# Two-layer graph kernel: 128 rows in each indirect transfer, the basis weight as innermost index, and seven instead of eight dense units in the middle stage

## What is computed

```python
h = relu(layernorm(x))
# layer 0: spline convolution, nine basis weights for each edge, mean over the edges of a destination
basis = hat(edge_attr[:, 0])[:, :, None] * hat(edge_attr[:, 1])[:, None, :]       # E x 9
msg = einsum("ek,ei,kio->eo", basis, h[src], weight)                               # E x 32
x = x + segment_sum(msg, dst) / max(degree, 1) + h @ root_w.T + root_b
# layer 1: graph attention with 8 heads (edges and self loops), then a dense block
h = relu(layernorm(x))
g = gat(h, src, dst)                       # softmax over the edges of a destination, mean of heads
y = layernorm(g + bias_gat + h)
x = x + layernorm(relu(y @ w1 + b1) @ w2 + b2 + y)
```

## Time and profile before

| | |
|---|---|
| median of 3 runs | 3093.12 us (3092.24 to 3096.14) |
| profiled execution, its own time | 3089.18 us |
| its span | 3087.3 us |
| granted TensorE clock, mean | 0.812 |
| busy: PE, PEld, DVE, ACT, POOL | 2138.2, 1492.6, 1802.5, 852.1, 2468.6 us |
| indirect transfers on POOL | 800 + 400 + 400 + 400 |
| software DMA queue (q0) | 64000 packets, 30.57 MB |
| hardware DMA queue (q1) | 52070 packets, 91.52 MB |

### The profile page before, as it was taken

One profiled execution on the slowest core, in us unless ns is written; L12 is line 12 of the kernel. 1 busy time (PEld: TensorE's weight loads), 2 busy tenths in 40 slices (PEclk: granted clock), 3 DMA queues, 4 the chain that ended last, 5 costly groups with the idle time before them and its releaser, 6 DMA issues.

```text
span 3087.3 us, 33471 instructions
## 1 busy us (share of the span) xinstructions
PE 2138.2 (69%) x10666; PEld 1492.6 (48%) x10666; DVE 1802.5 (58%) x3234; ACT 852.1 (28%) x1616; POOL 2468.6 (80%) x2011
## 2 busy tenths in 40 slices
PE   2777787756888878878887804876466877689710
PEld 1555555534666656556665503654333544355400
DVE  4889898995444444444444402444657689898600
ACT  1322233313333333333333302332111233123300
POOL 7777777777788888878788777788878888887877
PEclk9988898977878888888888856787577877899755
DMA  2333333331221222222121111111111111111100
GB/s 61 80 73 79 75 72 73 67 75 19 42 42 33 40 44 48 40 45 45 38 42 34 34 17 18 32 33 27 41 12 11 24 25 37 11 40 32 23 10 10
DMA packets 116219, 123.99 MB, mean 40 GB/s; under 512 B 70726, under 2 KB 72747, under 8 KB 116070
## 3 DMA queue, kind: packets, MB, share of 16 engines
q0 software_dynamic: 64000, 30.57, 10.6%
q1 hardware_dynamic: 52070, 91.52, 9.3%
HBM read 59.51 MB, written 64.00 MB: 40 GB/s over the span
## 4 chain that ended last, share of the span: by engine, by line
POOL 74%; issue 19%; DVE 4%; PE 2%; DMA 1%; POOLq 0%; ACT 0%; DVEq 0%
POOL ring L460 42%; POOL out_rows L508 16%; POOL x_table L482 16%; DVE region L1383 1%; PE V L598 1%; DVE region L1375 1%; DVE region L1311 0%; DVE region L1323 0%; PE T L525 0%; DMA ring<-in_x,index 0%; PE C L540 0%; DVE region L1320 0%; DMA ring<-x_table,index 0%; PE T L590 0%; DVE var L1280 0%
## 5 line engine op out<-in xcount | busy, mean ns | idle before, releaser
L460 POOL DMA_INDIRECT ring<-in_x,index x800 | 980.5, 1226 | 244.3 <-issue 244.0
L1280 DVE TENSOR_REDUCE var<-sq 125x16 f32<-125x512 f32 x325 | 221.4, 681 | 734.2 <-ACT sq L960 733.5
L508 POOL DMA_INDIRECT out_rows<-region,scatter_to x400 | 502.6, 1256 | 121.9 <-issue 121.9
L460 POOL DMA_INDIRECT ring<-x_table,index x400 | 496.3, 1241 | 124.4 <-issue 124.1
L482 POOL DMA_INDIRECT x_table<-region,index_out x400 | 486.3, 1216 | 124.4 <-issue 121.6
L564 PE MATMUL V<-xT,w_q 128*128 128x500 f32 x600 | 370.1, 755 | 25.1 <-ACT xT L952 24.0
L960 ACT ACTIVATE sq<-C 125x512 f32<-125x512 f32 x300 | 178.8, 596 | 729.0 <-PE C L576 422.4
L540 PE MATMUL C<-center,xT 128*125 128x128 f32 x1400 | 230.2, 317 | 90.0 <-ACT xT L952 47.8
L598 PE MATMUL V<-region,hT 128*125 128x384 f32 x600 | 255.3, 541 | 42.7 <-DVE region L1375 42.7
L540 PEld LDWEIGHTS C<-center,xT 128*125 128x125 f32 x1400 | 210.2, 224 | 154.3 <-issue 111.5
L576 PEld LDWEIGHTS C<-w_c,hid 128*125 128x125 f32 x2400 | 278.5, 195 | 0.0
(11 more groups left out here) (251 smaller groups left out, 3230.9 us busy)
## 6 DMA issues: line engine op xcount, KB each, us to landing
ring<-in_x,index POOLq DMA_INDIRECT x800, 3.1
nodes<-in_x SPq DMA_DIRECT2D x25, 500.0 KB
x_table<-nodes SPq DMA_DIRECT2D x25, 500.0 KB
x_plain<-nodes SPq DMA_DIRECT2D x25, 500.0 KB
nodes<-x_plain SPq DMA_DIRECT2D x50, 250.0 KB
out_rows<-nodes SPq DMA_DIRECT2D x50, 250.0 KB
x_table<-region,index_out POOLq DMA_INDIRECT x400, 2.6
ring<-x_table,index POOLq DMA_INDIRECT x400, 2.7
```

Of the source, the lines that this page charges most:

```text
L460: pool.indirect_dma_start(out=ring[0:P, j, s * F:(s + 1) * F], out_offset=None, in_=table, in_offset=bass.IndirectOffsetOnAxis(ap=index[0: ...
L508: pool.indirect_dma_start(out=out[:, :], out_offset=bass.IndirectOffsetOnAxis(ap=scatter_to[0:P, e:e + 1], axis=0), in_=diff[0:P, e * F:(e ...
L1280: v.tensor_reduce(unit(var, k), slots(squares(k)), AX.X, ALU.add).then_inc(var_ready, 1)
```

## The change

Three things change. First, every indirect DMA names 128 rows instead of 125. The three extra rows of each index array hold an index past the table (`index` and `index_out` are preset to N in partitions 96 to 127, `scatter_to` starts at N and above), and gathers now carry the bounds check too, so these rows are dropped. What the extra rows would read is set beforehand: `root_b` goes into three partitions of `ring` ahead of the gathers, and a load of x fills the three extra partitions of `region1`.

Second, in stage A the nine basis weights become the innermost index of weights, products and basis. A matmul now covers one slot: 288 columns (32 outputs x 9), four for each group. DVE has four products of 288 elements, and the sum over nine reads contiguous floats. The weight matrix is loaded in the old order into `w0_in` and copied into the new order once.

Third, a turn of the middle stage starts seven dense units instead of eight (`UNIT_AT`), so 35 units run there and 15 in stage D, over the waves 0 to 14.

```diff
+ROWS = 128
-N_BOOT = 6 * 4 + 2 + 2 + 2 + 4
+N_BOOT = 6 * 4 + 2 + 2 + 2 + 3
-UNIT_AT = (0, 1, 2, 4, 5, 6, 7, 9)
+UNIT_AT = (0, 1, 3, 4, 6, 7, 9)
-D_SLOTS = (8, 9, 6, 7)
+D_SLOTS = (7, 8, 9, 6)
...
@@ SP @@
+            sp.dma_start(ring[P:ROWS, :, :].rearrange("a j (s f) -> a (j s) f", f=F),
+                         root_b.rearrange("(a b f) -> a b f", a=1, b=1).to_broadcast([ROWS - P, NJ * CE, F])).then_inc(root_b_in, 16)
+            sp.wait_ge(index_set, 2)
...
-                load(w0_bd[q, :].rearrange("f (k t o) -> f k t o", k=KS, t=4)[:, :, t, :], w0.rearrange("k f o -> f k o"))
+                load(w0_in[q, :].rearrange("f (k t o) -> f k t o", k=KS, t=4)[:, :, t, :], w0.rearrange("k f o -> f k o"))
...
-            load(ring[P:P + 1, :, :].rearrange("a j (s f) -> a (j s) f", f=F),
-                 root_b.rearrange("(a b f) -> a b f", a=1, b=1).to_broadcast([1, NJ * CE, F]))
...
+            sp.dma_start(region1[P:ROWS, :], x_rows[0:ROWS - P, 0:TE * F]).then_inc(surplus_in, 16)
...
-                    for u in range(2, 4):
+                    for u in range(3, 4):
@@ GpSimd @@
-                        out=ring[0:P, j, s * F:(s + 1) * F], out_offset=None, in_=table,
-                        in_offset=bass.IndirectOffsetOnAxis(ap=index[0:P, j, s:s + 1], axis=0)).then_inc(ring_dma[j], 16)
+                        out=ring[0:ROWS, j, s * F:(s + 1) * F], out_offset=None, in_=table,
+                        in_offset=bass.IndirectOffsetOnAxis(ap=index[0:ROWS, j, s:s + 1], axis=0),
+                        bounds_check=last_row, oob_is_err=False).then_inc(ring_dma[j], 16)
...
+            pool.wait_ge(root_b_in, 16)
             gather_phase(x[:, :], 0, 0)
...
-                        out=x1_table[:, :], out_offset=bass.IndirectOffsetOnAxis(ap=index_out[0:P, j, s:s + 1], axis=0),
-                        in_=rows_out[0:P, j, s * F:(s + 1) * F], in_offset=None,
+                        out=x1_table[:, :], out_offset=bass.IndirectOffsetOnAxis(ap=index_out[0:ROWS, j, s:s + 1], axis=0),
+                        in_=rows_out[0:ROWS, j, s * F:(s + 1) * F], in_offset=None,
...
+            pool.wait_ge(surplus_in, 16)
             for c in range(NC):
...
-                        out=out[:, :], out_offset=bass.IndirectOffsetOnAxis(ap=scatter_to[0:P, e:e + 1], axis=0),
-                        in_=diff[0:P, e * F:(e + 1) * F], in_offset=None,
+                        out=out[:, :], out_offset=bass.IndirectOffsetOnAxis(ap=scatter_to[0:ROWS, e:e + 1], axis=0),
+                        in_=diff[0:ROWS, e * F:(e + 1) * F], in_offset=None,
@@ PE @@
-                    mm(V[bank][0:P, 0:3 * GF], hT[:, HE[j], g * P:(g + 1) * P], w0_bd[:, q * 3 * GF:(q + 1) * 3 * GF],
+                    mm(V[bank][0:P, 0:KS * F], hT[:, HE[j], g * P:(g + 1) * P], w0_bd[:, q * KS * F:(q + 1) * KS * F],
...
-                weigh(0, 1, 2)
+                weigh(0, 1, 2, 3)
...
@@ DVE @@
+            v.memset(index[96:ROWS, :, :], N).then_inc(index_set, 1)
+            v.memset(index_out[96:ROWS, :, :], N).then_inc(index_set, 1)
+            v.memset(region2[96:ROWS, 5904 + KS * GF:2 * H * TE + NJ * W], 0.0)
...
-                i = v.tensor_tensor(basis[0:P, :].rearrange("p (g k t) -> p g k t", k=KS, t=4)[:, :, k, :],
-                                    hat[:, 0, k // 3, :].rearrange("p (g t) -> p g t", t=4),
-                                    hat[:, 1, k % 3, :].rearrange("p (g t) -> p g t", t=4), ALU.mult)
+                i = v.tensor_tensor(basis[0:P, :].rearrange("p (s k) -> p s k", k=KS)[:, :, k],
+                                    hat[:, 0, k // 3, :], hat[:, 1, k % 3, :], ALU.mult)
...
+            v.tensor_copy(w0_bd.rearrange("p (t o k) -> p t o k", t=4, k=KS), w0_in.rearrange("p (k t o) -> p t o k", k=KS, t=4))
...
-                    for q in range(3):
+                    for q in range(4):
...
-                        to = (g % 2) * KS * GF + q * 3 * GF
-                        v.tensor_tensor(products[0:P, to:to + 3 * GF].rearrange("p (k o) -> p k o", o=F),
-                                        V[bank][0:P, 0:3 * GF].rearrange("p (k o) -> p k o", o=F),
-                                        basis[0:P, bass.ds((cv * G + g) * 4 * KS + q * 12, 12)].unsqueeze(2).to_broadcast([P, 12, F]),
+                        to = (g % 2) * KS * GF + q * KS * F
+                        v.tensor_tensor(products[0:P, to:to + KS * F].rearrange("p (o k) -> p o k", k=KS),
+                                        V[bank][0:P, 0:KS * F].rearrange("p (o k) -> p o k", k=KS),
+                                        basis[0:P, bass.ds((cv * CE + 4 * g + q) * KS, KS)].unsqueeze(1).to_broadcast([P, F, KS]),
...
-                                    products[0:P, (g % 2) * KS * GF:(g % 2 + 1) * KS * GF].rearrange("p (k c) -> p c k", k=KS),
+                                    products[0:P, (g % 2) * KS * GF:(g % 2 + 1) * KS * GF].rearrange("p (c k) -> p c k", k=KS),
```

More of the change, by code:

```diff
@@ L177, in gnn_program @@
         w0_bd = region2[:, 5904:5904 + KS * GF]
+        w0_in = products[:, 0:KS * GF]
         attr = region1[:, 0:800]
@@ L276, in gnn_program @@
         msgs_done = sem("msgs_done")
+        index_set = sem("index_set"); root_b_in = sem("root_b_in"); surplus_in = sem("surplus_in")
         block = ctx.enter_context(nc.Block())
@@ L441, in _ @@
             pool.memset(ident[:, :], 0.0).then_inc(boot_pe, 1)
-            pool.memset(w0_bd[:, :], 0.0).then_inc(boot_pool, 1)
+            pool.memset(w0_in, 0.0).then_inc(boot_pool, 1)
             pool.memset(root_bd[:, :], 0.0).then_inc(boot_pool, 1)
@@ L634, in a_wave @@
                 rows_T(2)
-                weigh(1, 1, 2)
+                weigh(1, 1, 2, 3)
                 t = center_rows(1)
@@ L638, in a_wave @@
                 centred(1, t); dense(2)
-                weigh(2, 1)
+                weigh(2, 1, 2)
                 t = center_rows(2)
-                weigh(2, 2); weigh(3, 0)
+                weigh(2, 3); weigh(3, 0)
                 centred(2, t)
-                weigh(3, 1, 2)
+                weigh(3, 1, 2, 3)
                 if jh is not None:
@@ L656, in _ @@
             with pe.Fori(0, NB - 1) as b:
-                tq.loop(b, 8 * NJ); cq.loop(b, 3 * NJ); vq.loop(b, 12 * NJ)
+                tq.loop(b, 8 * NJ); cq.loop(b, 3 * NJ); vq.loop(b, 16 * NJ)
                 st_t["h0"] = tq.base - lag_t; st.update({k: cq.base - lag for k, lag in lags.items()})
                 a_block(b + 1, False)
-                tq.end(NB - 1, 8 * NJ); cq.end(NB - 1, 3 * NJ); vq.end(NB - 1, 12 * NJ)
+                tq.end(NB - 1, 8 * NJ); cq.end(NB - 1, 3 * NJ); vq.end(NB - 1, 16 * NJ)
             st_t["h0"] = tq.base - lag_t; st.update({k: cq.base - lag for k, lag in lags.items()})
```

## The result

The changed kernel takes 2880.91 us (median of 4 runs, 2877.66 to 2883.55) against 3092.68 (3090.3 to 3096.14) for the kernel before on the same chip: a ratio of 0.9312, 95% interval 0.9301 to 0.9323. The direction was forecast, the size was not: 212 us were won where 347 were expected, and the time lies one microsecond above the top of the range. The profiled execution took 2880.49 us, with a span of 2878.7.

The account below looks back on a forecast made before the run. GpSimd's issuing of 2000 indirect transfers at 1.53 us was taken as the bound. Stretches of 654 + 964 + 24 + 638 + 448 + 24 gave 2752 us, 2733 at the lower price; forecast 2746, range 2660 to 2880.

Parts of the forecast that it names:

- The price of a transfer: GpSimd's instruction time per indirect transfer, about 1.2 us before: 128 rows would bring it to 0.8 to 1.0 us.
- p: Instruction plus gap of one indirect transfer on GpSimd: 1.53 us before, forecast 1.1 to 1.3.
- The sum at p = 1.3: All stretches of the kernel added: 654 + 964 + 24 + 638 + 448 + 24 = 2752 us.
- the middle with p = 1.1: Whole kernel, between the totals 2752 (p = 1.3) and 2733 (p = 1.1): 2742 us.
- A: First layer: DVE's saving of 62 us less 2 of boot moves its end from 714 to 654 us.
- Rival 4: Compute gives less: PE bounds A too (+30), or joins in D's waves 10 to 13 stretch (+50); 2775 to 2830; 0.14.
- B: Middle stage, to D's first gather: 24 us to the first scatter, 720 transfers 936, landing 4: 964 us.
- D: Stage of x1 gathers: compute 622 us, less 91 of gather waits, plus 107 of moved units: 638 us.
- The end: Last stage: 448 us of compute waiting for no indirect transfer, then the last sixteen scatters 21, landing 3.
- Small additions: Extra memsets and waits before the gathers, plus a surplus-row load: gathers start 3 to 6 us later; together 0 to 3.
- Rival 1: Issuing stays the bound at p from 1.35 to 1.49: 2827 us at 1.4, 2915 at 1.45; chance 0.13.
- Rivals 2 and 3: Transfer issuing: no effect, 3087 us, chance 0.06; or slower because rows and real descriptors cost more, 3150, chance 0.05.

Follow-up runs that it names:

- part 1 alone: The kernel before with only 128-row indirect transfers (old basis order, eight dense units): 2888.57 us, ratio 0.933; on two other chips 4239.35 and 4256.68 us.

## Why the prediction was wrong in size, step by step

**The price of a transfer** came out at the upper edge of its range. 0.8 to 1.0 us was forecast, 0.98 to 1.02 undisturbed came out, p = 1.30 and 1.33 with the disturbed ones (stage B: 720 transfers from 737.40 to 1696.7, 959 us). The prediction named a mean over 1.05 us as a sign of being wrong: three of the four groups are under it (1019, 1024 and 1040 ns), the output scatters at 1065 are not. The sum at p = 1.3 was the one to take; the middle with p = 1.1 was 10 us of hope. That GpSimd doesn't hold A's end also came true: its 480th gather ended at 677.0, and 60.45 us of idle followed. But it ended 43 us later than the 634 of the sum, 41 of them in waits for index loads; with A's end at 654 as in the sum, B's first scatter, at 678, would have found GpSimd only just free.

**A, "DVE's 62 us less 2 of boot put B's first gathered transpose at 654", is the step that failed.** DVE's busy time did fall by 60 us, the stage by 1.3. The windows of stage A, of after and of part 1 alone (length, busy us (x) of PE, PEld, DVE, ACT, POOL, granted clock, DMA share, GB/s):

```profile
90.00:712.00 622.00, 447.98 (x2444) 338.39 (x2442) 491.68 (x1051) 170.17 (x336) 418.86 (x420) 0.90 0.26 74
```

```profile
90.00:698.00 608.00, 452.74 (x2238) 307.79 (x2236) 548.88 (x951) 172.90 (x337) 417.53 (x419) 0.89 0.27 75
```

Nobody waits for gathers any more in either. With the old order DVE is busy 549 of 608 us; the new one takes 57 of them away and the window is 14 longer. The waits in the two windows, after first:

```profile
PE V L606 <- DVE region L1386: 140.3, 51, 12.0
...
DVE region L1386 <- PE V L606: 70.8, 108, 2.1
...
DVE var L1291 <- ACT sq L968: 41.5, 48, 2.2
```

```profile
PE V L606 <- DVE region L1386: 109.9, 27, 11.6
...
DVE region L1386 <- PE V L606: 41.0, 63, 1.5
...
DVE var L1291 <- ACT sq L968: 4.1, 3, 2.2
```

DVE's own waits grow by 30 and 37 us, which is the 57 saved and 10 more of the 14. The place is at the head of a wave. PE, then DVE, in a normal wave of after:

```profile
548.28 1.14 PE L606 MATMUL V<-region,hT 128*125 128x288 f32 x4
551.58 0.75 PE L606 MATMUL V<-region,hT 128*125 128x288 f32 x2 [2.17 <-DVE region L1386]
552.17 1.04 PE L548 MATMUL C<-center,xT 128*125 128x128 f32 x8
553.04 1.02 PE L594 MATMUL T<-nodes,ident_bias 126*125 126x512 f32 x2
553.90 1.04 PE L598 MATMUL T<-root_bd,hT 128*125 128x128 f32 x8
```

```profile
551.08 1.75 DVE L1386 TENSOR_TENSOR region<-V,region 125x288 f32<-125x288 f32 x4
553.87 0.69 DVE L1291 TENSOR_REDUCE var<-sq 125x16 f32<-125x512 f32 x1 [1.04 <-ACT sq L968]
555.53 0.46 DVE L1386 TENSOR_TENSOR region<-V,region 125x288 f32<-125x288 f32 x1 [0.98 <-PE V L606]
```

PE may run three products ahead of DVE, since the fourth V bank holds the scans' flags (`Uses(3)`, `cont_a`). A group used to be three products; now it is four. So PE sends three, stands 2.17 us until DVE has read the first, sends the fourth, and only then does the 3.1 us of centring and dense products, in which nothing reaches DVE's products. DVE then stands 1.04 us for the squares and 0.98 for its next product. In part 1 alone the same 3.1 us run before PE's wait, while DVE is in its two long reduces:

```profile
533.93 1.04 PE L598 MATMUL T<-root_bd,hT 128*125 128x128 f32 x8
536.68 0.91 PE L606 MATMUL V<-region,hT 128*125 128x384 f32 x2 [1.71 <-DVE region L1386]
```

Such a wave takes 19.3 us with the old order and 20.3 with the new, 1 us more although DVE has 2.4 us less to do. By PE's first transposes of the gathered rows, the five waves of a block take 31.8, 20.4, 20.3, 30.0 and 20.3 us with the new order and 32.9, 18.6, 19.3, 29.3 and 19.3 with the old: 3.4 us a block, 14 in four blocks, all of it in the waves without a scan. The lead and the place of the block are read from these rows and the code. A kernel with PE's block ahead of the fourth product, one with four banks, and one with part 3 and the old order were not run, so the mechanism is argued, its size (14.3 us at the seam) measured.

The clock is seen here too, but it is not what was lost. A wave with a scan holds DVE for 6.97 us in one piece, PE stands 9.30 us and comes back slower:

```profile
579.03 1.32 PE L606 MATMUL V<-region,hT 128*125 128x288 f32 x2 [9.30 <-DVE region L1386]
580.15 1.92 PE L548 MATMUL C<-center,xT 128*125 128x128 f32 x8
581.86 1.91 PE L594 MATMUL T<-nodes,ident_bias 126*125 126x512 f32 x2
```

The block takes 1.92 + 1.91 + 1.37 us here and 1.04 + 1.02 + 1.04 in the wave above; the granted clock is 0.56 from 579 to 585 and 1.00 in the wave above. So from 579 to 585 PE is mostly at the lower of its two levels, 1.2 GHz. Part 1 alone has the same pause and the same slow stretch behind it, 0.57 from 563 to 570; there it is the values that run slower:

```profile
563.15 1.64 PE L606 MATMUL V<-region,hT 128*125 128x384 f32 x2 [8.85 <-DVE region L1386]
```

The two waves with scans together are 0.4 us shorter with the new order, so the loss does not lie there.

The forecast gave A the whole of DVE's saving because DVE was its busiest engine. But DVE was busy 552 of 627 us and already tied to PE by 44.6 us of waits for its products; a saving on one of two engines in lockstep had to be checked against the order of the other. Rival 4 had half of the loss (+30), but with PE as the bound, and that is not what happened: PE is busy 448 of 622 us, not 475 + 20. The 20 us more of PE did not come, since its 1152 columns of a group took 245.4/100 = 2.45 us after and 249.2/100 = 2.49 in part 1 alone.

**B** came out at 986 for 964. p of 1.33 in place of 1.30 is 21 us of the 22. The compute did what was forecast: 37.9 us a chunk ((1647.0 - 736.4)/24), "about 38". It ended 50 us ahead of GpSimd's last scatter, so by an estimate 27 us of the relief are not used (its end, 1647, and 25 us for the last chunk's scatters and landing make 1672, not 1699).

**D** took 614 for 638. Waves 0 to 9 ran at 21 us, GpSimd's pace, units and all; waves 10 to 13, which carry the joins and now four units more, took 147.6 us (before 102.6), as rival 4 had it (+50). Against part 1 alone D is 61 us longer, not 107: the five units cost it 12 us each. Without them D took 553 us there, where the sum had 622 - 91 = 531. So the nearness of 614 to 638 is in part luck: a base 22 us too low and units 46 us too dear. PE's waits for gathers fell from 91.2 to 12.8 us, not to nothing.

**The end, "448 us of compute that waits for no indirect transfer; the last sixteen scatters 21, landing 3", is the second step that failed**, by 71 us. 13 of them are a misread row: 2936.42 in the earlier trace rows is the 24th chunk's last write, the 25th's ended at 2950.1, so compute took 460.6, and 460.8 after. The other 58 are scatters. The eleventh chunk is ready some 215 us after the last transpose (2335.43), and GpSimd starts on it at 2551.22. Fifteen chunks follow, 240 scatters at 1.33 us: 319 us to the last one's end at 2870.52. Compute needs only 245 us for the same chunks (last write 2796.2). So GpSimd is the bound in the last stretch even at the lower price, and 216 + 319 + 8 of drain is the 543 measured. DVE's last row is 74 us ahead of GpSimd's last, where some 20 were forecast. All of it could be read before: 15 x 16 x 1.3 = 312 us, against 246 from the eleventh chunk's finish to the last in the trace of before. The 8% of POOL in the chain that ended last is this stretch.

**Small additions** cost 1.6 us at GpSimd's first gather (3 to 6 forecast) and nothing that can be seen after it.

**The rivals.** Rival 1 (issuing the bound throughout, p from 1.35) was wrong in p, right in B and in the end, where GpSimd sets the time at 1.33. Rivals 2 and 3 fell. Rival 4's stretch of the joins came, its bound in A did not. The five terms together: 58.7 + 22.4 - 2.0 - 23.6 + 71.3 = 126.8 us above 2752.

## What to carry to other kernels

Count rows of an indirect transfer so that they divide by 16; 127 rows are dearer than 128 by 1.6 us. When the bound is lifted, follow its engine to the end of the program: a queue of finished work that starts late (here 240 scatters behind the eleventh chunk) keeps it the bound in that stretch. Before busy time saved on one of two engines in lockstep is counted, check the other's order and how far its buffers let it run ahead, above all when the number of pieces in a group grows past the buffers; here the saving was worth nothing.

## What the runs showed of the hardware that was not expected

- A gather of 125 rows with the bounds check costs some 0.07 us more than one without (1294 and 1226 ns). What the check costs at 128 rows was not run; there gathers of x and scatters of x1, both with it, are alike (1019 and 1024 ns).
- A gather's price is mostly its own: 0.90 us at 16 rows, 1.00 at 128. How the rows divide matters more than how many there are: 124 rows took 1.40 us, 127 took 2.61.
- Kernels with 128-row transfers took 4239 to 4311 us on two chips and 2878 to 2889 on the others used, the same kernel (part 1 alone) 4239, 4257 and 2889; the kernel before, with 125 rows, took 3091 to 3095 on all four of them. The changed kernel itself ran only on chips of the second kind. Whoever ships it should time it on more chips.
